# Message passing on a graph: the source nodes of two edge tiles in every 32 are not gathered from memory but copied out of SBUF, column by column

## The reference

```python
msg_in = concatenate([nodes[row], nodes[col], edge_features])        # 64 + 64 + 32
messages = relu(msg_in @ mW1 + mb1) @ mW2 + mb2                       # 128 hidden, 64 out
aggregated = segment_sum(messages, col)
x = layernorm(x + (relu(concatenate([nodes, aggregated]) @ uW1 + ub1) @ uW2 + ub2))
```

## Time and profile before

| | |
|---|---|
| time, median of 3 runs | 2034.05 us (2033.94 to 2034.74) |
| profiled execution, its own time | 2035.36 us |
| span of the profiled execution | 2033.6 us |
| mean granted TensorE clock | 0.785 |
| PE busy | 1408.9 us (69%) |
| DVE busy | 872.2 us (43%) |
| ACT busy | 557.6 us (27%) |
| POOL busy | 1488.3 us (73%), 1563 gathers |
| HBM read and written | 156.74 MB and 16.31 MB |

### The profile page before, as it was taken

How to read it: one execution, slowest core, us unless ns; L and a number is a source line. 1 busy time by engine, 2 the same in 40 slices (tenths; PEclk the granted TensorE clock), 3 DMA queues, 4 the chain that set the end, 5 groups by cost and what they waited for, 6 DMA issues and landing times.

```text
span 2033.6 us, 34717 instructions
## 1 busy us (share of the span) xinstructions
PE 1408.9 (69%) x10080; PEld 1283.7 (63%) x10080; DVE 872.2 (43%) x2225; ACT 557.6 (27%) x928; POOL 1488.3 (73%) x1576
## 2 busy tenths in 40 slices
PE   6777767666667676666766676767676767767775
PEld 6766666566666666666665565656665656656664
DVE  3543333333333333333334444444444444544444
ACT  4322222222222222222222232333233333333332
POOL 1777777777777777777777777777777777777774
PEclk8876777777777877787777877887787788787877
DMA  9732223322322322232222322323232323322321
GB/s 233 226 87 78 78 77 81 80 77 78 81 77 78 82 79 77 78 81 80 77 77 72 80 79 76 80 77 81 77 80 78 80 75 81 79 78 75 82 80 43
DMA packets 167906, 173.50 MB, mean 85 GB/s; under 512 B 65718, under 2 KB 129497, under 8 KB 167785
## 3 DMA queue, kind: packets, MB, share of 16 engines
q0 software_dynamic: 50016, 102.53, 19.4%
q1 hardware_dynamic: 104168, 63.40, 11.2%
q10 hardware_dynamic: 13698, 7.28, 1.6%
HBM read 156.74 MB, written 16.31 MB: 85 GB/s over the span
## 4 chain that ended last, share of the span: by engine, by line
POOL 69%; issue 24%; DMA 3%; PE 2%; POOLq 1%; DVE 0%; ACT 0%; SPq 0%; DVEq 0%; ACTq 0%
POOL ag L227 69%; DMA src_table<-ag 1%; PE bank L375 1%; DMA dst_table<-picks 1%; POOLq L213 0%; POOLq L224 0%; POOLq L785 0%; DMA xc<-x_t 0%; DMA dst_table<-hid 0%; PE bank L264 0%; PE bank L642 0%; PE bank L648 0%; PE bank L274 0%; DMA ag<-src_table,slot_idx 0%; DMA picks<-edge_t 0%
## 5 line engine op out<-in xcount | busy, mean ns | idle before, releaser
L227 POOL DMA_INDIRECT ag<-src_table,slot_idx x1563 | 1481.7, 948 | 521.5 <-issue 475.7
L274 PE MATMUL bank<-oh,hid 128*128 128x96 f32 x3128 | 532.5, 325 | 421.9 <-DVE xc L333 378.1
L274 PEld LDWEIGHTS bank<-oh,hid 128*128 128x128 f32 x3128 | 478.2, 234 | 481.0 <-ACT hid L295 428.4
L316 DVE TENSOR_TENSOR hid<-bank,ag 128x512 f32<-128x512 f32 x391 | 270.4, 692 | 897.0 <-DMA ag<-src_table,slot_idx 769.8
L264 PE MATMUL bank<-picked,picks 128*128 128x128 f32 x3128 | 583.2, 346 | 5.9 <-DMA picks<-edge_t 5.4
L295 ACT ACTIVATE hid<-hid 128x512 f32<-128x512 f32 x391 | 245.8, 629 | 1175.0 <-DVE hid L316 1175.0
L264 PEld LDWEIGHTS bank<-picked,picks 128*128 128x128 f32 x3128 | 521.2, 252 | 9.5 <-issue 5.9
L289 ACT ACTIVATE picks<-bank 96x512 f32<-96x512 f32 x391 | 226.6, 580 | 173.6 <-PE bank L251 131.4
L303 DVE TENSOR_TENSOR oh<-iota,rel 128x384 f32<-128x384 f32 x391 | 217.8, 557 | 118.9 <-PE bank L278 64.2
L251 PE MATMUL bank<-ident_bf,oh 128*96 128x128 bf16 x1564 | 194.2, 261 | 53.3 <-DVE oh L303 52.7
L251 PEld LDWEIGHTS bank<-ident_bf,oh 128*96 128x96 bf16 x1564 | 147.8, 155 | 104.1 <-DVE oh L303 66.2
(11 more groups left out here) (57 smaller groups left out, 327.8 us busy)
## 6 DMA issues: line engine op xcount, KB each, us to landing
picks<-edge_t SPq DMA_DIRECT2D x391, 64.0 KB
ag<-src_table,slot_idx POOLq DMA_INDIRECT x1563
picked<-dst_table SPq DMA_DIRECT2D x391, 48.0 KB
src_table<-ag SPq DMA_DIRECT2D x25, 256.0 KB, 4.2
dst_table<-picks SPq DMA_DIRECT2D x17, 256.0 KB, 4.6
xc<-x_t ACTq DMA_DIRECT2D x8, 400.0 KB, 15.3
resid<-x_rows SPq DMA_DIRECT2D x24, 128.0 KB
out<-resid ACTq DMA_DIRECT2D x24, 128.0 KB
```

Source lines behind the costliest of these rows:

```text
L227: pool.indirect_dma_start(out=ag[:, k, j * DH:(j + 1) * DH], out_offset=None, in_=src_table, in_offset=bass.IndirectOffsetOnAxis(ap=slot_i ...
L274: nc.tensor.matmul(ps_a[q][:, 0:WIN], hid[:, q, j * DH:(j + 1) * DH], oh[:, r, j * WIN:(j + 1) * WIN], start=(j == 0), stop=(j == TPG - 1))
L316: dve.tensor_tensor(hid[:, q, :], ps_h[q][:, :], ag[:, k, :], ALU.add).then_inc(s_pre, 1)
```

## The change

In each lap, tiles 2 and 3 of group k = 5 are no longer gathered (in laps 1 to 48; lap 0 gathers all). Their 256 source nodes are taken as columns of x out of `xc`, one at a time, into `own_x` (64 x 256), and `hidden` multiplies `own_x` with `w_src` and accumulates into the same PSUM bank; that is the same product of which `src_table` holds the result. The 256 columns are spread over the eight groups ahead of the one that uses them, 32 a group: at the end of its step DVE copies 16 of them and ACT 16 (`own_columns`). Each copy is of one column of 64 partitions and 4 bytes, and its place in `xc` is a register. Each of the two engines therefore loads 16 registers per group from a list of byte offsets in SBUF, which SP brings in two parts per lap from a scratch tensor in HBM (`load_own`); DVE multiplied that list by four at the start. `relu` at k = 5 reads the two tiles from PSUM, in an activation of their own.

The indices of the gathers are renewed by SP, four groups at once, with one transfer from HBM behind a wait for the gathers that last read those slots (`next_indices`); DVE's copy is gone. POOL waits for that transfer at k = 0 and k = 4, and otherwise for the `add_source` that freed the slot. DVE reads its window bases from a second copy, `base_lag2`, shifted by two words, so that its load starts at word 8i too.

```diff
@@ -37,6 +38,13 @@
 UPD_LAP = ITERS - CHUNKS + TAIL
 TB = 4
 TSTEPS = -(-BLOCKS // TB)
+OWN_K = 5
+OWN_TILES = 2
+OWN_AT = (TPG - OWN_TILES) * DH
+OWN = OWN_TILES * P
+OWN_N = OWN // UNROLL
+OWN_DVE = 16
+OWN_LATE = (UNROLL - OWN_K) * OWN_N
 XPARTS = 8
...
@@ -217,10 +238,74 @@
             return ap.bitcast(bf16).rearrange("p (n two) -> p n two", two=2)[:, :, 1]
-        def gather(pool, g, k, tiles=TPG):
-
-
-            wait(pool, s_idx, g - UNROLL + 1)
+        def gathered_of(k, lap):
+
+            return 16 * TPG + lap * 16 * gathered_tiles(k)
+
+        def gathered_tiles(k):
+
+            return TPG - OWN_TILES * (k == OWN_K)
+
+        def has_own(k, lap):
+
+            return k == OWN_K and not (isinstance(lap, int) and lap == 0)
+
+        def load_own(sp, k, lap):
+
+            last = isinstance(lap, int) and lap == ITERS - 1
+            if k == 1 and not (isinstance(lap, int) and lap == 0):
+                sp.wait_ge(s_own_dve, (lap - 1) * UNROLL + 1)
+                sp.wait_ge(s_own_act, (lap - 1) * UNROLL + 1)
+                sp.dma_start(own_early[:, :], own_dram[ds(lap, 1), OWN_LATE:]).then_inc(s_own_early, 16)
+            if k == OWN_K - 1 and not last:
+                if not (isinstance(lap, int) and lap == 0):
+                    sp.wait_ge(s_own_dve, (lap - 1) * UNROLL + UNROLL - OWN_K)
+                    sp.wait_ge(s_own_act, (lap - 1) * UNROLL + UNROLL - OWN_K)
+                sp.dma_start(own_late[:, :], own_dram[ds(lap + 1, 1), 0:OWN_LATE]).then_inc(s_own_late, 16)
+
+        def own_listed(eng, k, lap):
+
+            if k == OWN_K and not (isinstance(lap, int) and lap == ITERS - 1):
+                eng.wait_ge(s_own_late, (lap + 1) * 16)
+            elif k == 0 and not (isinstance(lap, int) and lap == 0):
+                eng.wait_ge(s_own_early, lap * 16)
+
+        def own_columns(eng, et, k, lap, a, b, copy, s_done):
+
+            step = (k - OWN_K) % UNROLL
+            last = isinstance(lap, int) and lap == ITERS - 1
+            if k >= OWN_K:
+                if last:
+                    return
+                row, at = own_late, step * OWN_N
+            else:
+                if isinstance(lap, int) and lap == 0:
+                    return
+                row, at = own_early, step * OWN_N - OWN_LATE
+            offsets = nc.values_load_multi_w_load_instructions(
+                row[0:1, at + a:at + b], engines=(et,), min_val=0, max_val=4 * (N_NODES - 1),
+                skip_runtime_bounds_check_because="four times the number of a node")[1]
+            for n, offset in enumerate(offsets):
+                c = step * OWN_N + a + n
+                done = copy(own_x[:, c:c + 1].bitcast(u8), xc[0:D, :].bitcast(u8)[:, ds(offset, 4)])
+            done.then_inc(s_done, 1)
+
+        def own_columns_dve(k, lap):
+
+            own_columns(nc.vector, ET.DVE, k, lap, 0, OWN_DVE, nc.vector.tensor_copy, s_own_dve)
+
+        def own_columns_act(k, lap):
+
+            def copy(to, of):
+                return nc.scalar.activation(to, of, ACT.Copy)
+            own_columns(nc.scalar, ET.Activation, k, lap, OWN_DVE, OWN_N, copy, s_own_act)
+
+        def gather(pool, g, k, lap, tiles=TPG):
+
+
+            if k % HALF == 0 and not (isinstance(lap, int) and lap == 0):
+                pool.wait_ge(s_idx[k // HALF], lap * 16)
+            wait(pool, s_pre, g - UNROLL + 1)
             pool.sem_inc(s_opened, 1)
             for j in range(tiles):
                 c = k * TPG + j
...
             wait(pe, s_pre, g - 1)
+            own = TPG - OWN_TILES if has_own(k, lap) else TPG
             for j in range(TPG):
                 last = nc.tensor.matmul(ps_h[q][:, j * DH:(j + 1) * DH], picks[:, r, j * P:(j + 1) * P],
-                                        picked[:, r, :], start=True, stop=True)
+                                        picked[:, r, :], start=True, stop=j < own)
+                if j >= own:
+                    if j == own:
+                        pe.wait_ge(s_own_dve, lap * UNROLL)
+                        pe.wait_ge(s_own_act, lap * UNROLL)
+                    last = nc.tensor.matmul(ps_h[q][:, j * DH:(j + 1) * DH],
+                                            own_x[:, (j - own) * P:(j - own + 1) * P],
+                                            w_src[0:D, :], start=False, stop=True)
             last.then_inc(s_h, 1)
         def aggregate(pe, g, k):
...
-        def relu(g, k):
+        def relu(g, k, lap):
             act = nc.scalar
             q = k % 2
             wait(act, s_pre, g + 1)
+            if has_own(k, lap):
+                act.activation(hid[:, q, OWN_AT:], ps_h[q][:, OWN_AT:], ACT.Relu)
+                act.activation(hid[:, q, 0:OWN_AT], hid[:, q, 0:OWN_AT], ACT.Relu).then_inc(s_relu, 1)
+                return
             act.activation(hid[:, q, :], hid[:, q, :], ACT.Relu).then_inc(s_relu, 1)
         def one_hot(g, k):
...
             missing = G_END * TPG - T_END if isinstance(g, int) and g == G_END - 1 else 0
-            wait(dve, s_gathered[k], (lap + 1) * 16 * TPG - 16 * missing)
+            wait(dve, s_gathered[k], gathered_of(k, lap) - 16 * missing)
             wait(dve, s_h, g + 1)
             wait(dve, s_agg, g - 1)
-            dve.tensor_tensor(hid[:, q, :], ps_h[q][:, :], ag[:, k, :], ALU.add).then_inc(s_pre, 1)
-
-        def next_indices(g, k):
-
-            dve = nc.vector
-            wait(dve, s_pre, g + 1)
-            dve.tensor_copy(slot_idx[:, k * TPG:(k + 1) * TPG],
-                            src_idx[:, ds((g + UNROLL) * TPG, TPG)]).then_inc(s_idx, 1)
+            w = OWN_AT if has_own(k, lap) else TPG * DH
+            dve.tensor_tensor(hid[:, q, 0:w], ps_h[q][:, 0:w], ag[:, k, 0:w], ALU.add).then_inc(s_pre, 1)
+
+        def next_indices(sp, k, lap):
+
+            if k % HALF != HALF - 1 or isinstance(lap, int) and lap == (ITERS - 1 if k == UNROLL - 1 else 0):
+                return
+            half, ahead = (0, 1) if k == UNROLL - 1 else (1, 0)
+            for slot in range(half * HALF, (half + 1) * HALF):
+                sp.wait_ge(s_gathered[slot], gathered_of(slot, lap + ahead - 1))
+            w = HALF * TPG
+            sp.dma_start(slot_idx[:, half * w:(half + 1) * w],
+                         src_all[:, ds((lap + ahead) * 2 * w + half * w, w)]).then_inc(s_idx[half], 16)
         def add_window(g, k, base):
...
+            row, at = (base_lag2, start + 2) if eng is ET.DVE else (base_row, start)
             return nc.values_load_multi_w_load_instructions(
-                base_row[0:1, ds(start, n)], engines=(eng,), min_val=0, max_val=LAST_BASE,
+                row[0:1, ds(at, n)], engines=(eng,), min_val=0, max_val=LAST_BASE,
                 skip_runtime_bounds_check_because="the chip clamps them to this range")[1]
...
@@ -779,14 +882,14 @@
...
             def windowed():
                 with pool.Fori(1, ITERS - 1) as i:
                     for k in range(UNROLL):
-                        gather(pool, i * UNROLL + k, k)
+                        gather(pool, i * UNROLL + k, k, i, gathered_tiles(k))
                 for g in range((ITERS - 1) * UNROLL, G_END):
-                    gather(pool, g, g % UNROLL, min(TPG, T_END - g * TPG))
...
             sp.dma_start(slot_idx[:, :], src_first).then_inc(s_first, 16)
...
             store_src_table(sp, range(4, 10))
-            sp.wait_ge(s_scratch, 64)
+            sp.wait_ge(s_own_4, 1)
+            sp.dma_start(own_dram, own_i).then_inc(s_scratch, 16)
+            sp.wait_ge(s_scratch, 80)
             sp.dma_start(base_all, base_f_dram[None, :].to_broadcast([P, GROUPS])).then_inc(s_back, 16)
             sp.dma_start(spread_row[:, :], spread_dram[None, :]).then_inc(s_back, 16)
             sp.dma_start(lag_row[:, :], lag_dram[None, :]).then_inc(s_back, 16)
             sp.dma_start(base_row[:, :], base_i_dram[None, :]).then_inc(s_back, 16)
+            sp.dma_start(base_lag2[:, 2:2 + GROUPS], base_i_dram[None, :]).then_inc(s_back, 16)
             store_src_table(sp, range(10, TSTEPS))
             sp.dma_start(src_idx[:, 0:TILES], src_all).then_inc(s_src, 16)
...
+                        load_own(sp, k, i)
+                        next_indices(sp, k, i)
                 lap(0)
...
                             act_square(c)
+                        own_listed(act, k, i)
                         if exists(g + 1):
                             copy_oh(g + 1, (k + 1) % UNROLL)
                         if c is not None and k == 6:
                             act_deviation(c)
                         if exists(g):
-                            relu(g, k)
+                            relu(g, k, i)
+                        own_columns_act(k, i)
                         if c is not None and k == 3:
                             act_relu(c)
                         if c is not None and k == 6:
...
                                      ).then_inc(s_base, 1)
+            dve.wait_ge(s_own, 16)
```

(34 more changed lines are left out.)

## The result

The changed kernel takes 2080.03 us (median of 4 runs, 2079.35 to 2080.72) against 2034.39 us before: the ratio is 1.0223, with a 95% interval of 1.0205 to 1.024. It is slower by 46 us, where 1931 us was forecast. The profiled execution took 2080.34 us, its span is 2078.6 us, the mean granted clock 0.800.

The account below looks back on a forecast made before the run. POOL's row of gathers was taken to bound the kernel: 2035.4 - 120.2 (gathers) + 11.5 (update laps) + 1.3 (indices) + 3.5 (start) + 1 (end) = 1932.5 us, 1931 against the median; range 1912 to 2090.

Parts of the forecast that it names:

- Gathers: On POOL, laps 1 to 48 lose two gathers each, 1.252 us apiece: 120.2 us gained, 37.6 us a lap.
- DVE's copies and loads: On DVE per group, 16 copies at 2.0 us and 16 register loads at 1.2 us; the group takes 4.0 us.
- The rival at 2730 us: DVE's 16 register loads take 3.9 us a group, a lap 54.6 us; part of the slower case, chance 0.30.
- The 1 us for bases and branch: On DVE, each lap pays 1 us for bases and branch beside 32 us of groups: 33 us, under 37.6.
- ACT's copies: On ACT, 16 copies take 2.2 us a group and registers 1.0 us; a group is 3.8 us, a lap 30.4.
- Start: Before the first gather, SP's storing and reading back of the offset list adds 3.5 us (0.5 to 6).
- Update laps: The 23 laps with a node update take 38.1 us, 0.5 over POOL's pace: +11.5 us (0 to 50).
- The wait that was priced: On ACT at k = 6 in update laps, relu's wait behind the deviation grows from 1.36 to about 4.5 us.
- The wait in `hidden` at k = 5: TensorE's hidden awaits both engines' copies of k = 4; add_source comes some 2 us late, DVE makes it up: 0.
- the one with update laps over POOL's pace: DVE or ACT sets the pace in update laps through dearer copies, loads or code: 2025 us, chance 0.24.
- registers or copies at their dearer bounds: The slower case: register loads at DVE's price, about 2730 us, or copies holding up gathers, 2040 us; chance 0.30.
- Indices by SP: SP's index transfers cost 1.3 us at the start only; dropping DVE's index copy saves 0.2 us a group.

Follow-up runs that it names:

- section 4: Follow-ups on the changed kernel with DVE's copies behind the update's parts: indices renewed by DVE's copy again, 2346.45 us; only DVE's wait behind add_source added, 2213.21 us.
- e1_dve_order: The changed kernel with DVE's 16 column copies moved behind the parts of the node update: 1934.01 us, ratio 0.9499 to the kernel before.
- Both edits: The changed kernel with DVE's copies behind the update's parts and TensorE's update matmuls behind the transpose and hidden: 1932.83 us, ratio 0.9506.
- the kernel with the hint: Branch-back hint on DVE's and ACT's loop of laps 1 to 25: added to e6_dve_order_dve_idx, 2267.86 us; added to e1_dve_order, 1942.71 us.
- e6_dve_order_dve_idx: e1_dve_order with the gather indices renewed by DVE's copy again instead of by SP: 2346.45 us, ratio 1.1544 to the kernel before.

## Why the prediction was wrong

- **Gathers:** right. 1467 are left, and plain laps take 37.7 us (forecast 37.6). A gather lasts 955 instead of 948 ns, some 10 us in all, which the sum did not have.
- **DVE's copies and loads:** right in the main. 16 copies take 682.9 / 384 = 1.78 us in the mean, less than the 2.0 taken, and a group 3.5 to 3.8 us against 4.0. The load has no row of its own; the 1.51 and 1.56 us of section 4 hold it, so 16 registers take at most some 1.5 us, 1.2 being taken, and the cover is full only where DVE's instructions run through without a wait. The rival at 2730 us needed 3.9 us for the load. The rule of the Trainium skill (Runtime: NRT & Kernel Launch, instruction fetch mechanics) that a register costs about 200 ns is not what these loads from SBUF show: 1.5 us for 16 is some 0.09 us each. The 1 us for bases and branch was wrong for plain laps, where DVE stands 4.24 us; POOL's pace covered that.
- **ACT's copies:** 634.1 us for 6144, 1.65 us for 16, against 2.2 taken. With the order mended, ACT's copies stay where they are and the update laps go at POOL's pace, so ACT is not the bound.
- **Start:** right in size. The first gather moves from 52.90 to the end of a wait of 49.2 instead of 45.4 us: 3.8, forecast 3.5.
- **Update laps:** this step failed. The working put "3.25 us more work and some waits" on DVE's lap and looked for a new wait at two places, `hidden` at k = 5 and `relu` at k = 6. At the place of the copies themselves it did not ask who waits for the instructions that now stand behind them. Those are `dve_c2` (L766) and `dve_stack` (L774); TensorE's L745 and L751 wait for them, ahead of the transpose and `hidden` in its program. In the changed kernel these two waits are 70.4 us (24 times) and 69.0 us (23 times), in e1_dve_order 22.9 and 22.1 us. That made an update lap 43.7 instead of 38.1 us. The 5.6 us x 23 laps = 129 us cover most of the 149 us between forecast and result; DVE's order gave back 146. The wait that was priced, of `relu` behind the deviation at k = 6, did not grow: ACT waits there 33.6 / 23 = 1.5 us before and 29.1 / 23 = 1.3 us after, where 4.5 was forecast, so the 11.5 us in the sum stood for something that did not happen. The wait in `hidden` at k = 5 came as forecast: DVE's `add_source` waits for it 78.2 / 48 = 1.6 us, where some 2 us were taken, and the plain laps still go at POOL's pace.
- **The rivals:** the one with update laps over POOL's pace had the right place and the wrong cause: not the price of a copy or of code, but a queue. It ended at 2025 us. That the 2080 us lie inside the stated range, 1912 to 2090, is no merit of it: the range reached up there for registers or copies at their dearer bounds, and neither came.
- **Indices by SP:** the price of L322 was wrong by far in one direction (279 us for its wait, once registers are loaded behind it), and gathers lengthened by up to 21 us in the other.

Moving the copies behind the update's parts makes of the change what the sum said: 1934.01 us, 5% faster than before. That this is so near the forecast 1931 is partly luck: the 11.5 us for update laps did not come (their pace is 30 x 300 / 239 = 37.7 us there), and gathers of 956 instead of 948 ns cost 1467 x 0.008, about 12 us, which the sum did not have. Both edits together give 1932.83 us, which is the best kernel here and not to be told from the first. More than two tiles a lap were not measured.

## What to carry to other kernels

When work is put into an engine's program at a fixed place, list what stands behind it on that engine, who waits for each of those instructions, and what is queued behind the waiter. Filler belongs behind the instructions that another engine waits for. A stretch in which several engines are less busy than in its neighbour, although they have more work there, and none is near full, hints at a circle of waits rather than a lack of throughput: look there for the first engine that stands idle before an instruction that isn't part of the main loop, and change the order alone to test it. And register work hides under an engine's running instructions only as far as no wait stands ahead of it; a wait for the engine's own last result is the worst, since what it waits for is what would have been the cover.

## What the hardware showed beyond what was expected

- A load of 16 registers left DVE no gap ahead of its copies where the instructions before ran through, one of 0.42 us where `add_source` had waited for a gather, and one of 0.84 us where DVE waited for `add_source`'s result. Over the kernel that is 129.4 against 325.7 us of idle time ahead of the copies, and 1934 against 2213 us.
- DVE stood still for 4.24 us at the start of a lap in the loop of laps 1 to 25, about 3 us of it for code by the kernel with the hint. In the second loop, whose body has the update as well, it stood only 1.1 to 1.3 us at the same place in nearly every lap, with the load of bases. In e6_dve_order_dve_idx, with one copy and one wait a group more on DVE, the second loop stalls too (3.7 to 4.0 us), and the packets of instructions are 369 instead of 265. So a small change of the code decides it; whether by its length or by its place was not tried.
- Gathers of POOL took 961 ns in the mean instead of 948 with the same gaps, after DVE's step had become shorter. A wait of DVE behind `add_source` brought them to 954 ns; the cause is open.
